# A fused routed-FFN, attention, routed-FFN block on one core: where the first gathers are issued, and in which pieces and order the attention's pipeline is filled

## The chip, the cores and the metric

The program runs on one core of a Trainium2 chip. The core has a matrix engine (TensorE, in the profile PE, its weight loads PEld), a vector engine (VectorE, DVE), an activation engine (ScalarE, ACT), GpSimd (POOL) and a queue engine (SyncE, SP). Each works through its own list of instructions in order and waits on semaphores. SP and ACT issue plain DMA transfers, POOL issues the indirect ones (gathers and scatters by row number). The metric is the device time of one execution in microseconds.

## The reference

The input x holds 32 sequences of 256 tokens of 128 numbers (8192 tokens). Three residual steps follow each other:

```python
x = x + 0.5 * ffn(layernorm(x), waff, W1, b1, W2, b2, threshold)
x = x + attn(layernorm(x), W_qkv, u_qkv, sigma_qkv, W_proj, u_proj, sigma_proj)
x = x + 0.5 * ffn(layernorm(x), waff, W1, b1, W2, b2, threshold)

# ffn: affinity of each token to 8 experts; one expert a token (argmax), kept where its
# rank within the sequence is below a capacity that comes from the mean affinity
dispatch = one_hot(argmax(aff)) * (ranks < cap)
for each expert: out += gelu((x * dispatch_e) @ W1_e + b1_e) @ W2_e + b2_e    # 128 -> 512 -> 128

# attn: 16 heads of 8, causal, softmax; weights scaled by spectral norms
qkv = sn_dense(x); att = softmax(mask(q k^T * 8**-0.5)); x = sn_dense(att v)
```

## The kernel before, in words

The program is a row of blocks: `token_stats` (layer norm statistics and affinities), `route("r1")` (which token goes to which slot), `experts("e1")`, `attention`, `experts("e2")`. At the end of a block every engine meets at a barrier (printed at the line of the block that comes next to it, here L496 for the end of `route`), then `Mem.clear` clears the semaphores and holds a second barrier (L66). No engine starts on the next block before both.

**The route and the first gathers.** VectorE makes in `gidx` the row numbers of 72 slot tiles (L798). POOL waits for it (`gidx_done`) and issues the gathers of the first two tiles (L577) within the `route` block. The rest of the tiles is gathered in `experts` (L867), in order on POOL. A tile is 128 rows of `rows`, two tiles are a pair and share one buffer `e_x`.

**The experts.** For pair i VectorE runs `keep(i)` (L1034, waits for both gathers of the pair), `norm` (L1045), and for each tile `fetch` (L1054), the copy of the tile's own expert's first weights into `e_w1own`. The list of VectorE holds `keep(5)` ahead of `fetch` for tile 6. TensorE transposes a pair (L972), expands each tile (L981), and contracts it (L992) some tiles later; ACT computes the gelu between (L936).

**The attention.** It is a pipeline over the 32 sequences in steps `turn(b)`, b from -4 to 35, each of twelve slots u = 0 to 11 on every engine. In turn b the work for several sequences is interleaved: sequence b+4 is gathered and normalised; sequence b+3 is projected to q and k (and v); the scores by query of sequence b+1 (its tiles 7 to 11, slots 0 to 4) and b+2 (its tiles 0 to 6, slots 5 to 11) are made for the row maxima only; for sequence b the scores by key are made, exponentiated (L1360), masked and multiplied by v. So the turns -4 to -1 fill the pipeline: turn -3 projects sequence 0, turn -2 projects sequence 1 and starts the maxima of sequence 0, turn -1 projects sequence 2, ends the maxima of sequence 0 and starts those of sequence 1, and turn 0 is the first with the scores by key.

The values q and k are carried as three bf16 parts. TensorE writes both to `mi[0]` (slot 2); ACT rounds them to the first part (L1371, `a_done`), VectorE takes the rest (L1697, `r_done`), ACT rounds it to the second part (L1380, `b_done`), and VectorE makes the third (L1711, `part_done`). SP then writes all of `part`, 192 KB in each of two transfers, to a buffer `qkd` in DRAM (L1226), and when they have landed reads it back in another layout: SP six transfers into `kb` (L1238), ACT six into `qs` (L1353). TensorE's first maxima tile of the sequence (L1430) waits for all twelve.

The row maxima of a sequence (VectorE's twelve reductions, L1678) are cut into three bf16 parts on POOL (L1328 to L1334), transposed on TensorE (L1552, slot 8, also in `mi[0]`), copied by ACT into `mt` (L1398) and written by SP into `qs` (L1231). The scores by key wait for that transfer (`m_in`).

In each turn SP holds, in this order: the transfers of `part` of sequence b+3, the maxima of sequence b+1, the reads into `kb`, and the rows of x.

## Time and profile before

| what | value |
|---|---|
| time, median of 3 runs | 1015.39 us (1014.93 to 1016.19) |
| profiled execution, its own time | 1012.83 us |
| its span | 1011.1 us |
| TensorE busy | 876.8 us, 87% of the span |
| VectorE busy | 748.7 us, 74% |
| GpSimd busy | 691.8 us, 68% |
| ScalarE busy | 599.8 us, 59% |

The busy time of an engine is the sum of its instructions without waits. The span is the part of the execution that the profiler records; the time of the execution includes what lies around it. In rows of the trace the first number is the start in microseconds from the span's start, the second the length; an `x6` behind a row says that six neighbours are merged, and square brackets give the idle time of the engine ahead of the row and what ended it.

### The profile page before, as it was taken

To read this page: it belongs to the slowest core of one execution; us is meant where nothing else is said; L and a number is where in the kernel's file an instruction comes from. 1 tells how busy PE (TensorE), PEld (TensorE's weight loads), DVE (VectorE), ACT (ScalarE), POOL (GpSimd) and SP (SyncE) were. 2 spreads that over 40 slices of the span, in tenths; PEclk is the share of its full clock that TensorE was granted. 3 is DMA by queue.
4 is the path that set the end of the run, shared out by engine and by line. 5 is a ranking of instruction groups with operands and counts; after the bars stand their busy time and mean duration, and the time that the engine had idled before them with its cause. 6 is when DMAs were issued, how large, how long until landed. Compare 5 with 4: busy or idle time off the path is not lost. (4 is left out here: it accounts for less than half of the span.)

```text
span 1011.1 us, 26251 instructions
## 1 busy us (share of the span) xinstructions
PE 876.8 (87%) x8024; PEld 664.9 (66%) x8057; DVE 748.7 (74%) x2500; ACT 599.8 (59%) x1575; POOL 691.8 (68%) x1245
## 2 busy tenths in 40 slices
PE   5936599999557999999999999999999974899995
PEld 5833499999524566565656566666666542899995
DVE  8879756555247789998998989898989854655552
ACT  2537466666314666666766666666666661666662
POOL 7709578753123678888888888888887774266664
PEclk9999889999858999999999999999999995899998
DMA  7450032222145553545464445455444301222220
GB/s 213 129 186 0 9 74 68 73 70 63 43 93 111 108 107 93 125 95 120 93 118 96 117 99 110 105 106 108 102 109 95 72 18 49 65 74 67 68 65 22
DMA packets 127017, 89.50 MB, mean 89 GB/s; under 512 B 14187, under 2 KB 117536, under 8 KB 126880
## 3 DMA queue, kind: packets, MB, share of 16 engines
q1 hardware_dynamic: 102752, 52.55, 22.9%
q10 hardware_dynamic: 15488, 17.74, 7.8%
q0 software_dynamic: 8640, 17.53, 6.7%
q8 instruction: 68, 1.11, 0.5%
q14 instruction: 69, 0.57, 0.2%
HBM read 52.09 MB, written 35.34 MB: 86 GB/s over the span
## 5 line engine op out<-in xcount | busy, mean ns | idle before, releaser
L1360 ACT ACTIVATE at_pt<-at_pm 128x512 f32<-128x512 f32 x384 | 228.0, 598 | 118.2 <-PE at_pm L1448 89.9
L1678 DVE TENSOR_REDUCE at_mx<-at_pp 128x2 f32<-128x512 f32 (+1 forms) x384 | 259.7, 679 | 43.0 <-PE at_pp L1437 35.7
L1276 POOL TENSOR_SCALAR_AFFINE_SELECT at_pt<-at_pt 128x256 f32<-128x256 f32 (+1 forms) x384 | 188.0, 493 | 57.1 <-ACT at_pt L1360 54.3
L936 ACT ACTIVATE e_ht<-e_ps_h,b1t 128x128 f32<-128x128 f32 x568 | 161.7, 370 | 84.2 <-PE e_ps_h L981 84.1
L981 PE MATMUL e_ps_h<-e_xnt,e_w1own 128*128 128x128 f32 x1136 | 153.3, 280 | 2.0 <-ACT e_xnt L930 1.3
L992 PE MATMUL e_ps_y<-w,e_ht 128*128 x1136 | 149.1, 275 | 0.0
L981 PEld LDWEIGHTS e_ps_h<-e_xnt,e_w1own 128*128 128x128 f32 x1136 | 141.0, 196 | 3.2 <-ACT e_xnt L930 2.0
L992 PEld LDWEIGHTS e_ps_y<-w,e_ht 128*128 128x128 f32 x1136 | 137.8, 192 | 0.0
L900 POOL DMA_INDIRECT out_dram<-e_y,e_x x71 | 82.3, 1159 | 68.1 <-DVE e_y L1062 51.9
L1062 DVE SCALAR_TENSOR_TENSOR e_y<-e_ps_y,e_x 128x256 f32<-128x256 f32 x72 | 30.3, 421 | 110.3 <-PE e_ps_y L992 110.3
L1469 PE MATMUL at_po<-at_pt,vp 128*32 128x256 f32 (+1 forms) x2048 | 109.8, 332 | 1.6 <-POOL at_pt L1276 1.6
L1435 PE MATMUL at_pp<-kb,qs 96*128 96x512 bf16 x256 | 100.1, 391 | 7.4 <-DVE at_mx L1678 6.2
L1448 PE MATMUL at_pm<-qs,kb 128*128 128x256 bf16 x512 | 97.7, 272 | 9.7 <-DMA qs<-at_mt 8.2
L867 POOL DMA_INDIRECT e_x<-rows,gidx x69 | 68.7, 995 | 38.8 <-DVE e_y L1062 21.3
L1469 PEld LDWEIGHTS at_po<-at_pt,vp 128*32 128x32 f32 x2048 | 53.4, 109 | 50.5 <-issue 21.0
L1448 PEld LDWEIGHTS at_pm<-qs,kb 128*128 128x128 bf16 x512 | 47.9, 97 | 48.1 <-DMA qs<-at_mt 15.5
L1322 POOL DMA_INDIRECT buckets<-at_x,at_to x64 | 65.4, 1022 | 20.0 <-issue 19.2
L1054 DVE COPY e_w1own<-w 128x512 f32 x142 | 64.7, 458 | 14.6 <-issue 9.3
L1283 POOL DMA_INDIRECT at_xa<-x,place x64 | 65.9, 1029 | 11.7 <-issue 11.3
L1437 PE MATMUL at_pp<-mask,identb 128*128 128x256 bf16 x256 | 70.9, 277 | 0.0
L1430 PE MATMUL at_pp<-kb,qs 96*128 96x256 bf16 x256 | 50.5, 279 | 7.6 <-DMA kb<-at_qkd 7.1
L1452 PE MATMUL at_pm<-qs,kb 128*128 128x128 bf16 x512 | 49.2, 218 | 2.8 <-ACT at_pt L1360 1.1
(324 smaller groups left out, 1744.5 us busy)
## 6 DMA issues: line engine op xcount, KB each, us to landing
at_qkd<-at_part SPq DMA_DIRECT2D x64, 192.0 KB, 3.0
kb<-at_qkd SPq DMA_DIRECT2D x64, 96.0 KB
qs<-at_qkd ACTq DMA_DIRECT2D x64, 96.0 KB
e_x<-buckets SPq DMA_DIRECT2D x71, 66.0 KB, 1.9
x<-e_y SPq DMA_DIRECT2D x35, 128.0 KB, 1.8
rows<-ts_x ACTq DMA_DIRECT2D x16, 264.0 KB, 3.0
ts_x<-in_x_dram SPq DMA_DIRECT2D x16, 256.0 KB, 3.3
x_by_token<-at_xa SPq DMA_DIRECT2D x32, 128.0 KB
```

The costliest lines, as they stand in the source:

```text
L867: pool.indirect_dma_start(x_row[s][:, j % 2, :], None, rows, bass.IndirectOffsetOnAxis(ap=c.gidx[:, j:j + 1], axis=0)).then_inc(x_in[s], 16)
L900: pool.indirect_dma_start(y_dram, bass.IndirectOffsetOnAxis(ap=to, axis=0), y_row[s][:, j % 2, :], None, bounds_check=T - 1, oob_is_err=Fa ...
L936: last = a.activation(hid_t[j % NB][:, f, :], ps_h[j % NB][:, f, :], ACT.Gelu, bias=c.b1t[:, ds(e, 1), f])
L981: last = te.matmul(ps_h[j % NB][:, f, :], w1_own[j % NB][:, f * P:(f + 1) * P], xn_t[(j // 2) % NX][:, j % 2, :], start=True, stop=True, s ...
L992: last = te.matmul(out, hid_t[j % NB][:, f, :], c.w2[:, ds(e, 1), f, :].rearrange("p a d -> p (a d)"), start=(f == 0), stop=(f == FC - 1))
L1276: g.affine_select(out=tile, in_=tile, compare_op=ALU.is_ge, fill=0.0, base=0, pattern=[[0, n], [1, P]], channel_multiplier=-1).then_inc(ma ...
L1360: a.activation(pt[u % RING][:, :], pm[u % 2], ACT.Exp, scale=SCALE).then_inc(exped, 1)
L1435: te.matmul(out, qs[s][0:ROWS, v - 4, P:S], kb[s][0:ROWS, v - 4, :, :].rearrange("p r q -> p (r q)"), start=True, stop=False, skip_group_c ...
L1437: te.matmul(out.rearrange("p (r q) -> p r q", r=2)[:, :, P:S], c.identb[:, :], c.mask[:, 0:2, :], start=False, stop=True, skip_group_check ...
L1448: last = te.matmul(out[:, i * S:(i + 1) * S], kb[s][:, g + 2 * w + i, r, 0:P], qs[s][:, g + 2 * w + i, :], start=True, stop=True)
L1469: last = te.matmul(out[32 * j:32 * j + 32, (half + 1) * S - cols:(half + 1) * S], values[:, w // 2, at:at + 32], src[:, i * cols:(i + 1) * ...
L1678: v.tensor_reduce(out, src, axis=AX.X, op=ALU.max).then_inc(maxed, 1)
```

## The change

Three things are changed, all of them at the start of a block.

First, the two gathers in `route` and their semaphore are gone, and `experts` issues all gathers.

Second, ACT makes one exponential of a single number at the very start of the attention's block. Nothing uses its value.

Third, the fill is ordered differently. For sequence 0 alone, `part` is written in pieces: the first parts when `a_done` is there, the second parts at `b_done`, the third parts at `part_done`, the last of these six transfers issued by ACT. Up to turn 0 VectorE makes the third parts ahead of the maxima tile in slot 5. In turn -1 the maxima of sequence 0 are transposed at the start of slot 5 instead of in slot 8, are copied by ACT in slot 5, and SP writes them ahead of the parts of sequence 2.

```diff
-            pool.wait_ge(gidx_done, 1)
-            for j in range(2 * HEAD_PAIRS):
-                pool.indirect_dma_start(c.x_row[j // 2][:, j % 2, :], None, io["rows"], ...)
...
-                for j in range(2 * HEAD_PAIRS, 2 * NR):
+                for j in range(2 * NR):
                     gather(j)
...
+            def maxima_in(b, k):
+                q = (k + 1) % NQ
+                wait(sp, mt_out, b + 2)
+                sp.dma_start(qs[q][ROWS:ROWS + 6, :, :], mt[q % 2][:, :].unsqueeze(1)).then_inc(m_in[q], 16)
...
+                    if n == 0:
+                        for done, s in ((a_done, slice(0, 6, 5)), (b_done, slice(1, 5, 3))):
+                            wait(sp, done, 1)
+                            for r in range(2):
+                                sp.dma_start(rows_out(h, r)[:, s, :], part[h][64 * r:64 * r + 64, s, :]).then_inc(piece_out, 16)
+                        wait(sp, part_done, 1)
+                        sp.dma_start(rows_out(h, 0)[:, 2:4, :], part[h][0:64, 2:4, :]).then_inc(part_out[h], 16)
+                    if b == -1:
+                        maxima_in(b, k)
+                    if n > 0:
+                        wait(sp, part_done, n + 1)
...
+            a.activation(cell[0:1, 7:8], c.part[0:1, 0:1], ACT.Exp, scale=-1.0).then_inc(early_exp, 1)
             act.wait_ge(zeroed, NZ)
...
+                    if u == 8 and b == -3:
+                        wait(act, part_done, 1)
+                        act.dma_start(rows_out(0, 1)[:, 2:4, :], part[0][64:P, 2:4, :]).then_inc(part_out[0], 16)
-                    if u == 8 and has(1):
+                    if u == (5 if b == -1 else 8) and has(1):
...
+                        if b == -1:
+                            wait(pe, mt_out, b + 2)
...
+                    if b == -1 and u == 5:
+                        wait(pe, r_done, b + 4)
+                        turn_maxima()
...
+                    if u == 5 and has(3) and b < 1:
+                        third_pieces(b, k)
                     for o, w in QUERY_TILES[u]:
```

On POOL, at the border of `route` and `experts`, the list before reads (L577 is in `route`, L496 and L65 are the border):

```order
L573 TENSOR_SCALAR qs<-r_iotab,r_colp 128x128 x48
L577 DMA e_x<-rows,gidx 128x132 x2
L496 UNCONDITIONAL_BRANCH
L65 ISA
L863 UNCONDITIONAL_BRANCH
L867 DMA e_x<-rows,gidx 128x132 x22
```

and now:

```order
L573 TENSOR_SCALAR qs<-r_iotab,r_colp 128x128 x48
L496 UNCONDITIONAL_BRANCH
L65 ISA
L859 UNCONDITIONAL_BRANCH
L863 DMA e_x<-rows,gidx 128x132 x24
```

The two gathers stand behind the border instead of ahead of it.

On TensorE, in turn -1 (kb0 and qs0 are sequence 0, kb1 and qs1 sequence 1, at_mp0 the cut maxima of sequence 0), before:

```order
L1435 MATMUL at_pp1<-kb0,qs0 128x512
L1437 MATMUL at_pp1<-mask,identb 128x2x128
L1430 MATMUL at_pp0<-kb1,qs1 128x256 x2
L1432 MATMUL at_pp0<-mask,identb 128x512
L1525 MATMUL at_mi0<-wv,at_xt0 128x128 x2
L1430 MATMUL at_pp1<-kb1,qs1 128x256 x2
L1432 MATMUL at_pp1<-mask,identb 128x512
L1430 MATMUL at_pp0<-kb1,qs1 128x256 x2
L1432 MATMUL at_pp0<-mask,identb 128x512
L1430 MATMUL at_pp1<-kb1,qs1 128x256 x2
L1432 MATMUL at_pp1<-mask,identb 128x512
L1552 MATMUL at_mi0<-identb,at_mp0 48x128 x2
```

and now:

```order
L1455 MATMUL at_pp1<-kb0,qs0 128x512
L1457 MATMUL at_pp1<-mask,identb 128x2x128
L1497 MATMUL at_mi0<-identb,at_mp0 48x128 x2
L1450 MATMUL at_pp0<-kb1,qs1 128x256 x2
L1452 MATMUL at_pp0<-mask,identb 128x512
L1554 MATMUL at_mi0<-wv,at_xt0 128x128 x2
```

The transposes of the maxima moved from behind four tiles of sequence 1 to ahead of the first.

On SP, in the attention's fill (kb0 to kb2 are the buffers of sequences 0 to 2, at_qkd0 and at_qkd1 the two DRAM buffers), before, without the reads of sequences 0 and 1 that stand between:

```order
L1226 DMA at_qkd0<-at_part0 64x6x256 x2
L1238 DMA kb0<-at_qkd0 24x8x256
...
L1226 DMA at_qkd1<-at_part1 64x6x256 x2
L1238 DMA kb1<-at_qkd1 24x8x256
...
L1241 DMA x1_by_token<-at_xa0 128x2x128
L1226 DMA at_qkd0<-at_part0 64x6x256 x2
L1231 DMA qs0<-at_mt0 6x8x256
L1238 DMA kb2<-at_qkd0 24x8x256
```

and now:

```order
L1231 DMA at_qkd0<-at_part0 64x2x256 x4
L1233 DMA at_qkd0<-at_part0 64x2x256
L1252 DMA kb0<-at_qkd0 24x8x256
...
L1241 DMA at_qkd1<-at_part1 64x6x256 x2
L1252 DMA kb1<-at_qkd1 24x8x256
...
L1255 DMA x1_by_token<-at_xa0 128x2x128
L1218 DMA qs0<-at_mt0 6x8x256
L1241 DMA at_qkd0<-at_part0 64x6x256 x2
L1252 DMA kb2<-at_qkd0 24x8x256
```

Sequence 0 goes out in five transfers from SP (the sixth is ACT's), and in turn -1 the maxima of sequence 0 and the parts of sequence 2 have changed places.

## Rows read from the trace of the kernel before

**Rows 1.** Stretches: start:end, length, busy time by engine (instructions), PEclk, DMA share, GB/s

```profile
310.00:316.50 6.50, 5.67 (x21) 1.84 (x20) 5.82 (x15) 0.45 (x2) 0.72 (x1) 0.50 0.45 110
333.50:337.00 3.50, 2.11 (x27) 1.42 (x20) 1.89 (x4) 2.10 (x5) 2.42 (x4) 1.00 0.44 97
440.00:800.00 360.00, 341.97 (x3502) 219.22 (x3524) 326.15 (x993) 240.10 (x520) 302.01 (x653) 1.00 0.49 105
```

**Rows 2.** Line L496, drains at the end of `route`: min/median/max ns, first and last start

```profile
L496 POOLq DRAIN  x1: 4502/4502/4502, 118.2 to 118.2; - x1
L496 DVEq DRAIN  x1: 10/10/10, 118.9 to 118.9; - x1
```

**Rows 3.** Timeline, start of the experts

```profile
124.12 0.95 POOL L867 DMA_INDIRECT e_x<-rows,gidx  x1 [3.14 <-POOLq L66]
125.23 0.14 DVE L1034 TENSOR_TENSOR e_x<-e_x,keep 128x2 f32<-128x2 f32 x1
128.72 3.78 PE L981 MATMUL e_ps_h<-e_xnt,e_w1own 128*128 128x128 f32 x16 [0.83 <-ACT e_xnt L930]
```

**Rows 4.** Timeline, the sixth pair in the experts

```profile
136.24 0.94 POOL L867 DMA_INDIRECT e_x<-rows,gidx  x1 [0.30 <-issue]
138.79 0.17 DVE L1034 TENSOR_TENSOR e_x<-e_x,keep 128x2 f32<-128x2 f32 x1 [1.35 <-DMA e_x<-rows,gidx]
138.90 0.43 DVE L1054 COPY e_w1own<-w 128x512 f32 x1
139.40 0.74 PEld L981 LDWEIGHTS e_ps_h<-e_xnt,e_w1own 128*128 128x128 f32 x6
```

**Rows 5.** Timeline, turns -3 and -2 of the attention

```profile
280.32 0.60 ACT L1371 ACTIVATE at_part<-at_mi 128x512 bf16<-128x512 f32 x1 [2.17 <-PE at_mi L1488]
282.33 0.69 DVE L1711 TENSOR_TENSOR at_part<-at_rest,at_part 128x512 bf16<-128x512 f32 x1 [0.69 <-ACT at_part L1380]
283.06 1.35 SPq L1226 DMA_DIRECT2D at_qkd<-at_part  x2
286.70 4.48 SPq L1238 DMA_DIRECT2D kb<-at_qkd  x6
293.33 0.63 ACT L1380 ACTIVATE at_part<-at_rest 128x512 bf16<-128x512 f32 x1 [0.76 <-DVE at_rest L1697]
294.31 0.61 PE L1430 MATMUL at_pp<-kb,qs 96*128 96x256 bf16 x2 [2.37 <-DMA kb<-at_qkd]
296.69 1.31 SPq L1226 DMA_DIRECT2D at_qkd<-at_part  x2
```

**Rows 6.** DMA issues of the page: KB each, median us from issue to landing

```profile
at_qkd<-at_part SPq DMA_DIRECT2D x64, 192.0 KB, 3.0
e_x<-buckets SPq DMA_DIRECT2D x71, 66.0 KB, 1.9
```

**Rows 7.** Timeline, turn -1 and the start of turn 0

```profile
306.24 0.68 DVE L1678 TENSOR_REDUCE at_mx<-at_pp 128x2 f32<-128x512 f32 x1
307.88 0.24 POOL L1334 TENSOR_TENSOR at_mp<-at_nr,at_mp 128x32 bf16<-128x32 f32 x1
310.29 1.31 SPq L1226 DMA_DIRECT2D at_qkd<-at_part  x2
313.89 4.32 SPq L1238 DMA_DIRECT2D kb<-at_qkd  x6
318.37 0.40 PE L1452 MATMUL at_pm<-qs,kb 128*128 128x128 bf16 x4 [0.92 <-ACT at_pt L1360]
321.28 0.11 PEld L1430 LDWEIGHTS at_pp<-kb,qs 96*128 96x128 bf16 x2 [0.69 <-DMA kb<-at_qkd]
```

**Rows 8.** Timeline, table load and SP in turn 0, a wait in turn 1

```profile
316.43 1.28 ACT L1360 ACT_TABLE_LOAD   x1 [3.71 <-issue]
326.40 0.81 SPq L1231 DMA_DIRECT2D qs<-at_mt  x1
335.82 0.11 PEld L1430 LDWEIGHTS at_pp<-kb,qs 96*128 96x128 bf16 x2 [1.61 <-DMA kb<-at_qkd]
```

More of the change, by code:

```diff
@@ L546, in route @@
         zeroed = sem("zeroed")
-        far_done, near_done, gidx_done = sem("far"), sem("near"), sem("gidx")
+        far_done, near_done = sem("far"), sem("near")
         NA = 2
@@ L1472, in times_v, with turn_maxima @@
                     last.then_inc(pv_done, 1)
+                def turn_maxima():
+                    wait(pe, mp_done, b + 2)
+                    for j in range(TPB):
+                        last = te.transpose(mi[0].bitcast(BF16)[0:3 * H, j * P:(j + 1) * P],
+                                            mp[(k + 1) % 2][:, j, :, :].rearrange("p t h -> p (t h)"), c.identb[:, :])
+                    last.then_inc(mt_tr, 1)
                 def small(u):
@@ L1659, in _, with third_pieces @@
             dve.wait_ge(made, NM)
+            def third_pieces(b, k):
+                q = (k + 1) % 2
+                wait(dve, b_done, b + 4)
+                v.tensor_tensor(part[q][:, 2:4, :], rest[q][:, :].rearrange("p (a n) -> p a n", a=2), part[q][:, 1:5:3, :],
+                                ALU.subtract).then_inc(part_done, 1)
             def turn(b, k, has):
@@ L1707, in turn @@
                                         ALU.mult).then_inc(on_done, 1)
-                    if u == 5 and has(3):
-                        q = (k + 1) % 2
-                        wait(dve, b_done, b + 4)
-                        v.tensor_tensor(part[q][:, 2:4, :], rest[q][:, :].rearrange("p (a n) -> p a n", a=2), part[q][:, 1:5:3, :],
-                                        ALU.subtract).then_inc(part_done, 1)
+                    if u == 5 and has(3) and b >= 1:
+                        third_pieces(b, k)
                     if u == 6 and has(4):
```

36 lines of the change are left out of this document (16 added, 20 removed).

## The prediction

> **What bounds the kernel now.** I read the stretches first, then the chain of waits, then the timeline at the borders of the blocks. In the steady part of the attention TensorE is busy 341.97 of 360 us at its full clock, and VectorE 326.15 [rows 1]. In the experts TensorE's instructions stand back to back. So whatever starts the experts or the attention earlier shifts all that follows by as much, as long as TensorE is not starved a moment later; and an instruction that is removed in the steady part is not what this change is about. The change works on two borders: the end of the route, and the attention's fill (turns -4 to 0), where TensorE waits for transfers several times.
>
> At the end of the route VectorE is the last to compute; its drain stands at 118.9. POOL's drain starts at 118.2 and lasts 4.50 us, to 122.7: it holds the barrier until the gathers that POOL has issued are through [rows 2]. In the fill the chain runs from the parts of a sequence (SP's write) through DRAM to the reads into `kb`, to TensorE's first maxima tile. TensorE is found waiting for `kb` at 294.31, 321.28 and 335.82 [rows 5, 7, 8].
>
> **Part one, the gathers.** Removed from the route: two gathers on POOL, and with them the long drain. The barrier is then VectorE's: 118.9 in place of 122.7, so all engines enter the experts 3.8 us earlier. Added in the experts: the same two gathers, ahead of the fourteen others that are issued without a wait. One gather follows another after 0.94 + 0.30 = 1.25 us [rows 4]. POOL's first one moves from 124.12 [rows 3] to 120.3; the third, which was the first there, comes 2 x 1.25 later, at 122.8. So each later gather is 3.8 - 2.5 = 1.3 us earlier.
>
> Who waits for them? The first pair: its second gather ends at 120.3 + 1.25 + 0.94 = 122.5, and a gather's data is there 1.6 us after that (136.24 + 0.94 to 138.79 [rows 4]), so at 124.1. Before, `keep` for the first pair ran at 125.23, held by VectorE's own start and not by data [rows 3]. Thus TensorE's first expansion, at 128.72 before, could start up to 2.3 us earlier. But not all of it lasts. At 138.79 `keep(5)` waited 1.35 us for its gathers, the copy of tile 6's weights stands behind it on VectorE and ends at 139.33, and TensorE takes that tile at 139.40 [rows 4]: a margin of under 0.1 us. This wait now comes 1.3 us earlier, not 2.3, and TensorE waits for the difference. After this pair POOL gains on TensorE (2.5 us a pair against four tile steps of 0.9, some 3.8), so nothing further is lost. Part one: **-1.3 us**. The ends of its range: -0.9 if the two gathers, which come first in a block, take 0.2 us more each (my allowance), and -2.3 if the wait at `keep(5)` gives way.
>
> **Part two, the fill.** I take the times in the frame of before, with the attention's start fixed.
>
> *Pieces of sequence 0.* Before, both transfers wait for the third part: issued from 283.06 on over 1.35 us, landed at 286.70 when the reads begin [rows 5], 2.9 us after the second's start. Now the first parts are ready at 280.92 and the second at about 282.3 (where the third begins) [rows 5]. The trace shows no transfer of this shape. Its issue on SP is bounded by 0.81 us for the 24 KB of maxima [rows 8] and 0.68 for 192 KB (half of 1.35), 0.75 for a read (a sixth of 4.48) [rows 5]; below I allow 0.4, since a third of the runs of data is left. At 0.65 SP issues from 280.96 to 282.25, from 282.35 to 283.65, and the last at 283.65; ACT's comes beside it. That is hardly earlier than the second transfer before (283.73); the rest must come from size. A 66 KB read lands in 1.9 us, a write of 192 KB in 3.0 [rows 6]. With 2.15 us for a write of 64 KB, nearer to the row of its size, the reads start at 285.8: **-0.9 us**, between -0.2 (it lands no faster for being small) and -1.2 (issues at 0.4 us).
>
> A rule speaks against this. The Trainium skill, "DMA: Bandwidth & Descriptors", section "Rules for kernel authors", says that many small transfers should be joined, since under 64 KB one pays mostly overhead; its section on the anatomy of one DMA puts the fixed part at about 2.0 us plus bytes over 436 GB/s. By that estimate a piece of 64 KB lands in 2.15 us and one of 192 KB in 2.45, a gain of only 0.3; the rows have 1.1 us between the two sizes, and the sum goes by the rows.
>
> *Third parts first.* In turn -2 the second part of sequence 1 is ready at 293.96, but its write starts at 296.69 [rows 5], because VectorE first had the maxima tile that waits for `kb`. Now the write starts at 293.96 - 0.9 + 0.75 = 293.85, which is 2.8 us earlier. The tile behind it on VectorE arrives on TensorE only at 294.31 - 0.9, so the 0.68 us of the third part cost nothing. The reads for sequence 1 land 2.8 us earlier too, and ACT, which issues six of them, is free sooner for the copy of sequence 2.
>
> *Maxima in turn -1.* They end at 306.92 before, the cutting on POOL at 308.12 [rows 7]. What leads to them starts with TensorE's first tile of sequence 0 (-0.9) and runs through ACT, now unblocked: -1.1, so the cut maxima are there at 307.0. TensorE now waits for them ahead of the first tile of sequence 1, whose reads, issued from 297.45 on and as long on the way as those of sequence 0 (7.6 us), have landed at about 305.1. So what the reads gain is not all used: queued behind the transposes are the seven tiles of sequence 1, and they start at 307.45. ACT copies at 307.5, SP writes at 307.95 for 0.8 us, and only then, at 308.75, the parts of sequence 2, in place of 310.29 [rows 7]: **-1.5 us**, although they were ready at 306.6. The reads of sequence 2 start at 312.35 (before 313.89).
>
> *Turn 0.* The first scores by key come 1.8 us earlier. The table load of 1.28 us ahead of the first exponential [rows 8] now lies at the attention's start, where ACT does nothing until the first copy of sequence 0; together with ACT's earlier reads TensorE's step at 318.37, which waited for ACT, comes 2.8 us earlier. But the next tile that needs new data, at 321.28, already waited 0.69 us for `kb` [rows 7]; its data is 1.5 us earlier and no more. TensorE waits there 1.7 us instead, and of the 2.8 us 1.5 are left. So the early table costs nothing and by itself yields nothing: the wait for the reads of sequence 2 takes its place. In turn 0 SP reads sequence 3 only after the write of sequence 1's maxima, which ended at 327.21 [rows 8] and follows TensorE, also -1.5; the wait of 1.61 us at 335.82 stays as it is. Part two: **-1.5 us**, from -0.8 (pieces at -0.2) to -2.8 (the read of sequence 2 is not what binds).
>
> **Sum.** -1.3 - 1.5 = -2.8 us: the profiled execution goes from 1012.83 to 1010.0. The median of the runs is 2.56 us above that execution, so 1015.39 becomes **1012.6**.
>
> **Rivals.**
>
> *A, the gains are real but half as large* (chance 0.2). The two gathers cost 1.45 us each and the pieces land no faster than the whole: -0.9 - 0.8 = -1.7, giving 1013.7. For it: the pieces' last issue is at the time of the old one. Against it: the 1.1 us between the sizes.
>
> *B, TensorE isn't held by the next wait* (0.15). `keep(5)` slips by less, and the reads land earlier because the DMA engines are less crowded: -2.3 - 2.8 = -5.1, giving 1010.3. Against it is the margin of 0.1 us at 139.40; for it, that the six reads of sequence 0 needed 7.6 us from issue to the first tile and those of sequence 2 7.4, under a load that may change.
>
> *C, the clock falls in turn 0 and the kernel is slower* (0.1). From 310 to 316.5 TensorE was granted 0.50, that is 1.2 GHz of 2.4, after TensorE had sat idle for the reads of sequence 1 [rows 1]. The new wait of 1.7 us at 319 follows soon on the slow stretch. If the clock stays low there, every slow microsecond costs half: 6.5 us cost 3.3, and the result is 1015.39 - 2.8 + 3.3 = 1015.9. It decides against the change from 5.6 us of slow clock on, and needs 9.7 for a loss that counts. Against it: a wait of 1.61 us at 335.82 left the clock at 1.00 [rows 1, 8].
>
> *D, the whole fill is hidden* (0.05): TensorE is short of work in turns 1 and 2 anyway and gives all of part two back; 1014.1.
>
> **The numbers.** My own case has 0.5, with a range of 1011.8 to 1013.6. All cases but the far ends of B and C lie between 1010.5 and 1014.9, the edge on the slow side reaching past A and D. A measurement of this kernel tells about 0.2% (2.0 us) from no change. My case gives faster in nine of ten, B always, A and D scarcely, C never, which with D's and A's remainder gives 0.65 faster, 0.28 the same, 0.07 slower, the last from C and from what I have not seen.
>
> **What would show it.** POOL's drain at the route's end under 1 us and the first gather near 120.3; the first expansion near 126.4, then a wait of about 1 us of TensorE ahead of tile 6, held by the sixth pair's gathers. In the attention, counted from its start: reads of sequence 0 0.9 us earlier, the write of sequence 1 2.8, of sequence 2 1.5; no table load in turn 0; a longer wait for `kb` in turn 0. I would be wrong if the barrier does not follow VectorE, if the pieces land together as late as before, if TensorE's clock in turn 0 is below 1, or if the distance from turn 0 to the attention's end grows.

## The result, and the profile after

The changed kernel takes 1012.05 us, the median of 13 runs (1008.74 to 1014.03), and the kernel before 1015.39 (13 runs, 1013.31 to 1017.54). The ratio of the two is 0.9970, with a 95% interval of 0.9961 to 0.9980. On another chip the same pair gave 1012.73 and 1015.54, ratio 0.9971, interval 0.9961 to 0.9982 (e12 below). So the change makes the kernel 2.8 to 3.3 us faster; 2.8 had been forecast. The profiled execution of the changed kernel took 1011.68 us with a span of 1009.9.

Positions are compared below as distances from an event that both kernels have: in the experts from the end of the last instruction that VectorE computes in the route (the cast into `eid`: 118.64 before, 119.33 after), in the attention from POOL's first gather into `at_xa` (270.73 before, 270.04 after). Such a distance is written with a plus sign, +14.96. Line numbers differ between the kernels.

**The border of the route.** The drains of L496 in the changed kernel, which answer to [rows 2] (count, min/median/max ns, first and last start):

```profile
L496 POOLq DRAIN  x1: 9174/9174/9174, 102.5 to 102.5; - x1
L496 DVEq DRAIN  x1: 10/10/10, 119.6 to 119.6; - x1
```

POOL's drain is not shorter, it is longer: 9.17 us. But it begins at 102.5, while POOL's last work of the route (L573) is still running, and ends at 111.7, as that work does, well ahead of VectorE. What counts is when a drain ends, not how long it is. The barrier is now VectorE's.

The start of the experts and the sixth pair in the changed kernel, which answer to [rows 3] and [rows 4]:

```profile
120.32 1.28 ACT L936 ACT_TABLE_LOAD   x1 [7.04 <-PEq L66]
121.11 1.24 POOL L863 DMA_INDIRECT e_x<-rows,gidx  x1 [9.47 <-POOLq L66]
123.92 0.94 POOL L863 DMA_INDIRECT e_x<-rows,gidx  x1 [0.30 <-issue]
125.30 0.16 DVE L1030 TENSOR_TENSOR e_x<-e_x,keep 128x2 f32<-128x2 f32 x1 [3.17 <-DMA e_x<-rows,gidx]
127.16 1.22 PE L977 MATMUL e_ps_h<-e_xnt,e_w1own 128*128 128x128 f32 x4 [0.47 <-ACT e_xnt L926]
...
135.46 0.95 POOL L863 DMA_INDIRECT e_x<-rows,gidx  x1 [0.31 <-issue]
138.14 0.16 DVE L1030 TENSOR_TENSOR e_x<-e_x,keep 128x2 f32<-128x2 f32 x1 [1.51 <-DMA e_x<-rows,gidx]
138.26 0.43 DVE L1050 COPY e_w1own<-w 128x512 f32 x1
138.79 0.91 PE L977 MATMUL e_ps_h<-e_xnt,e_w1own 128*128 128x128 f32 x6 [0.72 <-ACT e_xnt L926]
```

Read the releasers. `keep` for the first pair is now held by its gathers for 3.17 us, where before VectorE's own start held it. TensorE's first expansion stands at +7.83 in place of +10.08, 2.25 us earlier. At tile 6 TensorE sits idle for 0.72 us, and there was no such gap before. The row names ACT's copy of `e_xnt` as the releaser, but the copy of tile 6's weights ends at 138.69, only 0.1 us ahead of TensorE, and it stands behind `keep(5)`, which waited 1.51 us for gathers. From here on to the attention everything is 1.3 to 1.4 us earlier: the attention starts at +150.71, before at +152.09.

Look at POOL as well. The third gather starts at +4.59 (123.92), before at +5.48 (124.12): 0.89 us earlier. The twelfth, the last that `keep(5)` needs, starts at +16.13 (135.46), before at +17.60 (136.24): 1.47 us earlier. The difference of 0.58 us is not made by the change: the nine gathers between, the same in both kernels, took that much less in this profile.

**The fill of the attention.** Timeline of the changed kernel, which answers to [rows 5], [rows 7] and [rows 8]:

```profile
269.27 1.28 ACT L1358 ACT_TABLE_LOAD   x1 [5.67 <-PEq L66]
280.25 2.63 SPq L1231 DMA_DIRECT2D at_qkd<-at_part  x4
282.36 0.68 ACTq L1413 DMA_DIRECT2D at_qkd<-at_part  x1
282.92 0.61 SPq L1233 DMA_DIRECT2D at_qkd<-at_part  x1
285.00 4.56 SPq L1252 DMA_DIRECT2D kb<-at_qkd  x6
292.65 0.69 DVE L1692 TENSOR_TENSOR at_part<-at_rest,at_part 128x512 bf16<-128x512 f32 x1 [0.69 <-ACT at_part L1397]
293.37 1.30 SPq L1241 DMA_DIRECT2D at_qkd<-at_part  x2
...
304.95 0.73 DVE L1692 TENSOR_TENSOR at_part<-at_rest,at_part 128x512 bf16<-128x512 f32 x1
306.53 0.27 PE L1497 MATMUL at_mi<-identb,at_mp 128*48 128x128 bf16 x2 [3.27 <-POOL at_mp L1348]
306.73 0.39 PE L1450 MATMUL at_pp<-kb,qs 96*128 96x256 bf16 x2
307.24 0.78 SPq L1218 DMA_DIRECT2D qs<-at_mt  x1
308.12 1.32 SPq L1241 DMA_DIRECT2D at_qkd<-at_part  x2
311.74 4.34 SPq L1252 DMA_DIRECT2D kb<-at_qkd  x6
313.48 0.63 PE L1468 MATMUL at_pm<-qs,kb 128*128 128x256 bf16 x2
...
319.41 0.39 PE L1450 MATMUL at_pp<-kb,qs 96*128 96x256 bf16 x2 [1.41 <-DMA kb<-at_qkd]
333.28 0.11 PEld L1450 LDWEIGHTS at_pp<-kb,qs 96*128 96x128 bf16 x2 [0.28 <-DMA kb<-at_qkd]
```

The last piece of sequence 0 is issued at 282.92 and the reads begin at 285.00: 2.1 us, where the whole half took 2.9. The third part of sequence 1 is ready ahead of the maxima tile, and its write follows at once. In turn -1 a new gap appears, the one that matters most below: TensorE waits 3.27 us for the cut maxima at 306.53, and SP holds back the parts of sequence 2, ready at 305.68, until 308.12. The first tile of sequence 1 stands at 306.73 (+36.69, before +37.60), the first scores by key at 313.48 (+43.44, before +44.52). The same stretches as in [rows 1], the first two moved to the same distance from the attention's start:

```profile
309.31:315.81 6.50, 6.22 (x25) 2.62 (x26) 5.52 (x14) 1.21 (x3) 1.14 (x2) 0.55 0.65 145
332.81:336.31 3.50, 3.44 (x39) 2.47 (x38) 2.65 (x6) 2.59 (x6) 2.72 (x6) 1.00 0.16 41
440.00:800.00 360.00, 340.98 (x3504) 220.03 (x3526) 325.89 (x996) 241.16 (x522) 302.30 (x652) 1.00 0.48 105
```

The steady part is as before. The half clock in the first stretch is still there in this profile (0.55, before 0.50), and the clock does not fall in turn 0.

A caution on the end. The table load of the last experts stands 588.44 us behind the attention's start, before 588.74: of a fill that is 1.5 us shorter this pair of profiles shows 0.3 at the end. The steady turns differ by more than that from one execution to the next. The reads of the last sequence stand at +515.98, +519.08 and +517.44 in the three profiles with the old fill (before, e1, e3; mean 517.5), and at +515.06, +516.61, +516.06, +516.70 and +516.54 in five with the new one (after, e2, e4, e9, e12; mean 516.2). The means differ by 1.3 us, but the three old ones alone spread over 3.1, so the profiles point to a gain that is carried to the end and do not show it by themselves. The times do: the fill alone has a ratio below 1 over its whole interval (e2), if only just. For single steps I rely on positions in the fill, and on times only where an interval speaks. The positions spread too: the reads of sequence 2 stand at +43.16, +43.70 and +44.84 in the three profiles with the old fill, and at +41.70 to +42.04 in the five with the new one. Against the profile of before the gain there is 1.46 us, between the means 2.0.

### The profile page after: what moved, and what is told of

It reads as the page before. It is cut to its first block and busy times, and to the rows that moved or that the text cites. A ratio compares the mean times of both kernels' runs of the same rounds, so it can differ in the third digit from the quotient of the medians.

```text
span 1009.9 us, 26259 instructions
## 1 busy us (share of the span) xinstructions
PE 876.5 (87%) x8024; PEld 665.2 (66%) x8057; DVE 748.7 (74%) x2500; ACT 600.8 (59%) x1576; POOL 691.7 (68%) x1245
```

## The experiments

All times are device microseconds. The ratio is to the kernel before on the same chip, with its 95% interval. Three chips were used: e1 to e4 ran on one (before: 1016.29), e5 to e8 on a second (1027.81), e9 to e12 on a third (1015.54). On the second the profiles show TensorE, ACT and VectorE standing still for some 12 us in all in the first experts, much of it released by nothing that the profile shows, and the kernel before took 12 us longer there too; positions counted from the attention's start don't contain it.

### e1: the gathers alone

The kernel before with part one only (no gathers in `route`, all 24 in `experts`).

> The kernel before with only the gathers moved into the experts. Theory (the barrier follows VectorE, then the sixth pair's gathers hold TensorE): POOL's drain at the route's end under 0.1 us, all engines in the experts 3.7 us earlier, the first expansion 2.1 us earlier counted from the end of the route's last VectorE instruction, tile 6 only 1.3 us earlier, and the attention's start 1.3 us earlier; time -1.3 us (ratio 0.9987). Rival B (TensorE is not held at tile 6): the attention's start 2.1 to 2.3 us earlier. Rival that the barrier's gain is void: no shift. The attention's fill has the positions of before, counted from its start.

Measured: 1015.79 us, ratio 0.9993 (0.9982 to 1.0004). ACT's first instruction of the experts stands at +1.00, the first expansion at +7.82, the gap at tile 6 is 0.65 us, and the attention starts at +150.87 in place of +152.09: 1.22 us earlier. Up to the attention's start the positions agree with the theory, but the third gather is 0.90 us earlier and not 1.3 (+4.58); the twelfth, at +16.43, is 1.17 earlier. The fill does not have the positions of before, as was expected: it is unchanged, and yet its write of sequence 1 comes 0.81 us later than in the profile of before, its reads of sequence 2 1.68 later, and those of sequence 6 3.0. That is the spread spoken of above. The time can't tell 1.2 us from nothing.

### e2: the fill alone

The kernel before with the parts two and three of the change.

> The changed kernel with the two gathers back in the route: only the fill's edits are left. Theory: the experts as before (tile 6 without a wait), the attention's positions those of the changed kernel: the first read of sequence 0 1.0 us earlier counted from the attention's start, of sequence 2 1.4, the wait for kb in turn 0 about 1.4 us. If the fill lasts, time -1.5 us (0.9985); if the later turns take back what they took in the profile of the changed kernel, -0.9 us.

Measured: 1015.08 us, ratio 0.9987 (0.9975 to 0.9999). The experts are as before (first expansion +10.07, attention +152.10). Reads of sequence 0 at +15.03, write of sequence 1 at +23.30, reads of sequence 2 at +41.98, of sequence 3 at +55.88. The fill of the changed kernel is reproduced without the experts' part. By the positions the two parts are independent; the two ratios multiply to 0.9980, against 0.9970 measured for both, each uncertain by 0.0010 to 0.0012, so the times allow it and no more.

### e3: one gather left in the route

```diff
-            for j in range(2 * HEAD_PAIRS):
+            for j in range(1):
...
-                for j in range(2 * HEAD_PAIRS, 2 * NR):
+                for j in range(1, 2 * NR):
```

> The kernel before with one gather in the route and the other in the experts. It parts the two things that come with the first edit: the earlier start of the block, and the place of the gathers in POOL's list. POOL's drain should end 1.25 us earlier, and so should the experts' start; but POOL then has one more gather there, so that all gathers from the third on stand where they stood. Theory (the gathers set TensorE's time at tile 6): tile 6 and the attention's start are unmoved within 0.2 us, time 0. Rival (the block's start sets it): 1.25 us earlier, ratio 0.9988.

Measured: 1017.39 us, ratio 1.0000 (0.9988 to 1.0011). L496 in this kernel:

```profile
L496 POOLq DRAIN  x1: 3179/3179/3179, 118.3 to 118.3; - x1
```

With one gather in flight the drain is 3.18 us, with two 4.50 [rows 2]: each gather adds about one gather's issue, and in both the drain ends 1.7 us after the record of the last gather. The engines enter 1.3 us earlier than before, the first expansion is 1.3 earlier (+8.76), but POOL still has to issue the gather that it gave up, so that the third gather is where it was (+5.42, before +5.48). The attention starts at +151.71, 0.38 us earlier, where 0.2 at most was expected by the theory and 1.25 by the rival. That is far nearer to the theory, and the rest has a likely source: the twelfth gather came 0.57 us earlier (+17.03), because the gathers ahead of it were shorter. So what counts in the end is the time of the sixth pair's gathers, not the time at which the engines enter.

### e4: the weights of tile 6 ahead of keep(5)

The changed kernel, with `fetch(6)` taken out of its place behind `keep(5)` and put ahead of it:

```diff
+                if by_slot and i == 1:
+                    fetch(6, e[6])
                 if i + NORM < NU:
                     keep(i + NORM)
```

> The changed kernel with the copy of tile 6's weights ahead of the wait for the sixth pair's gathers on VectorE, in the first experts only. Theory: TensorE's wait of 0.72 us at tile 6 is due to that order alone; it goes, TensorE's later tiles and the attention's start come 0.7 us earlier, time -0.7 us against the changed kernel. Rival: the sixth pair's rows themselves are needed as soon (the transposes of the pair wait): the wait moves to the next transposes and nothing is gained.

Measured: 1014.24 us, ratio 0.9979 (0.9966 to 0.9992). The gap at tile 6 is gone, and the transposes of the sixth pair come at +22.57 in place of +23.10. But the attention starts at +151.27, not earlier than +150.71. The loss is at the tenth pair. Timeline of e4, POOL, VectorE and TensorE, and then the same place in the changed kernel:

```profile
152.50 2.14 DVE L1050 COPY e_w1own<-w 128x512 f32 x1
152.53 1.83 POOL L873 MEMSET kb<- 96x2048 f32 x1
154.75 1.13 PE L977 MATMUL e_ps_h<-e_xnt,e_w1own 128*128 128x128 f32 x8 [0.68 <-issue]
```

```profile
151.70 1.83 POOL L873 MEMSET kb<- 96x2048 f32 x1
152.63 1.19 DVE L1050 COPY e_w1own<-w 128x512 f32 x1
...
155.99 1.82 POOL L873 MEMSET kb<- 96x2048 f32 x1
156.78 1.31 DVE L1050 COPY e_w1own<-w 128x512 f32 x1 [0.27 <-issue]
```

A copy of this shape takes 0.42 us. These take 2.14, 1.19 and 1.31, and each ends 0.28 to 0.29 us after the memset that POOL is running. VectorE's copy and POOL's memset don't overlap: the copy is held until the memset is through. In e4 the copy is wanted 0.03 us ahead of the memset by the records, and loses all of it. (The Trainium skill, "SBUF — State Buffer", section "Who interferes with whom", states such a lock between VectorE's instructions in a two-port mode and GpSimd, held for a whole instruction by whoever issues first. The rows agree on the lock; on the order they show a copy with the earlier start waiting. Whether this copy runs in such a mode, no trace here says.) So a wait was removed and given back 16 us later, by a collision that the new time brought about.

### e5: sequence 0 written whole

The changed kernel, with the write of sequence 0 as before (two transfers of 192 KB at `part_done`).

> The changed kernel, but sequence 0 is written as before, in two transfers of 192 KB when the third parts are there. Counted from the attention's first gather, the changed kernel's pieces are written from 10.21 to 12.88 and its reads begin at 14.96, those of before at 15.97. Theory of the prediction (a small write lands sooner): reads of sequence 0 at 15.9 to 16.0, first maxima tile about 1.0 later, and so the write of the maxima and of sequence 2's parts about 1.0 later (39.1); the attention ends 1 us later. Rival (the pieces buy nothing downstream, because the cut maxima come from ACT and VectorE, which have slack): reads later by 1.0, but sequence 2's parts within 0.3 of 38.08.

Measured: 1026.81 us, ratio 0.9992 (0.9979 to 1.0005). Timeline of e5 (its attention starts at 282.53):

```profile
298.58 4.48 SPq L1243 DMA_DIRECT2D kb<-at_qkd  x6
306.57 0.61 PE L1436 MATMUL at_pp<-kb,qs 96*128 96x256 bf16 x2 [2.77 <-DMA kb<-at_qkd]
```

Reads at +16.05 in place of +14.96, the first maxima tile at +24.04 in place of +22.72, the maxima of sequence 0 at +38.91 in place of +37.20, the reads of sequence 2 at +43.43 in place of +41.70. Within the fill the theory holds, and the rival (slack downstream) does not: the loss of 1.1 us at the reads is still there in turn -1. That it grows to 1.7 is not the edit's doing alone. In e7 and e8, whose fill is that of the changed kernel up to there, the last maxima tile of sequence 0 also comes 1.0 us later on this chip (+33.7 in place of +32.73). Beside e6, the profile of this chip nearest to the changed kernel, the loss is 0.97 at the reads of sequence 0, 1.31 at the maxima and 1.32 at the reads of sequence 2. That the attention ends 1 us later is not seen: at the reads of sequence 4 the loss against e6 is 0.1 (e6 has a stop of its own ahead of them), and the last sequence, at +515.78, stands where it does in the changed kernel. The chip has no run of the changed kernel beside it, so only the positions speak here.

### e6: without the early exponential

> The changed kernel without the early exponential: the table is loaded ahead of the first exponential again (1.28 us). Theory of the prediction: the first exponential comes 1.3 later than 44.25, the wait of TensorE for kb at 49.4 shrinks from 1.7 to about 0.4 or less, and what follows that tile stands where it was: 0 us. Rival (the table load is on the path): the tile itself slips by 1.28 and with it all that follows: +1.3 us.

The one line with `early_exp` is left out. Measured: 1026.31 us, ratio 0.9987 (0.9975 to 0.9999). Timeline of e6 (its attention starts at 282.97):

```profile
328.08 1.28 ACT L1376 ACT_TABLE_LOAD   x1 [5.70 <-issue]
332.92 0.11 PEld L1449 LDWEIGHTS at_pp<-kb,qs 96*128 96x128 bf16 x2 [0.68 <-DMA kb<-at_qkd]
```

The first exponential comes at +46.40 in place of +44.25 to +44.61, the wait of TensorE for `kb` shrinks to 0.68 us from 1.69 to 2.09, and the tile that ends it stands at +49.95; in the profiles of after, e2, e9 and e12 it stands at +49.36, +49.90, +49.90 and +49.76. What the table load costs, the wait for the reads gives back, all but a few tenths: the early table yields next to nothing, as predicted. (Turn 1 of this profile is then 1.0 to 1.6 us later, behind one stop of TensorE of 1.51 us at +65 that the profile puts down to nothing, as those in the experts on this chip.)

### e7: the maxima of turn -1 late again

The changed kernel, with the transposes of the maxima in turn -1 in slot 8 and SP's write of them behind the parts of sequence 2, as before the change. Pieces, early third parts and early table stay.

```diff
-                    if b == -1:
-                        maxima_in(b, k)
...
-                    if b == -1 and u == 5:
-                        wait(pe, r_done, b + 4)
-                        turn_maxima()
```

> The changed kernel, but in turn -1 the maxima of sequence 0 are transposed in slot 8 and written behind the parts of sequence 2, as before. Theory (the reads of sequence 2 bind turn 0, and SP writes the maxima ahead of them in either order): parts of sequence 2 written at about 35.7 in place of 38.08, maxima only at 39.5 to 41, so the reads of sequence 2 at 40.5 to 41.8 (changed kernel 41.70), the first scores by key 1.5 to 2.5 later than 43.44; TensorE waits less for kb, and the tile of sequence 2 comes within 0.5 of the changed kernel's 51.05: 0 us, so that the third part ahead of the tile alone brings what the write order seems to bring. Rival (early maxima are what shortens the fill): everything from turn 0 on 1.3 us or more later.

Measured: 1024.72 us, ratio 0.9978 (0.9965 to 0.9990), the lowest on its chip. Timeline of e7 (its attention starts at 281.83):

```profile
316.81 0.39 PE L1448 MATMUL at_pp<-kb,qs 96*128 96x256 bf16 x2 [0.76 <-DMA kb<-at_qkd]
318.49 1.30 SPq L1239 DMA_DIRECT2D at_qkd<-at_part  x2
320.99 0.81 SPq L1218 DMA_DIRECT2D qs<-at_mt  x1
322.10 4.31 SPq L1250 DMA_DIRECT2D kb<-at_qkd  x6
323.49 0.39 PE L1466 MATMUL at_pm<-qs,kb 128*128 128x256 bf16 x2
329.75 0.39 PE L1448 MATMUL at_pp<-kb,qs 96*128 96x256 bf16 x2 [1.95 <-DMA kb<-at_qkd]
```

The maxima are written 2.0 us later (+39.16), a little ahead of what was expected. But the first scores by key come at +41.66, which is 1.8 us **earlier** than in the changed kernel (+43.44), and the reads of sequences 2, 3 and 4 at +40.27, +53.89 and +68.97 in place of +41.70, +55.34 and +70.47. Neither the theory (no change) nor the rival (later) had this. The reads of sequence 2 come earlier because SP no longer waits for the maxima ahead of the parts: these are written at +36.66 in place of +38.08. The scores come earlier because TensorE starts the seven tiles of sequence 1 at +34.98 in place of +36.69, 1.71 us earlier: nothing in its queue waits for the maxima any more. It also runs them at the full clock. The stretch of 6.5 us from +39.27 in e7 (the granted clock is the third number from the right):

```profile
321.10:327.60 6.50, 5.57 (x33) 2.81 (x32) 5.32 (x10) 2.71 (x6) 2.38 (x5) 1.00 0.69 139
```

A pair of matmuls takes 0.39 us here, and 0.61 to 0.64 from the third tile on in the changed kernel, where this stretch was granted 0.55. But the clock explains next to nothing here. From the first tile of sequence 1 to the first scores it takes 6.68 us in e7 at the full clock, 6.75 in the changed kernel, 6.69 in e8 at 0.50, and 6.89 in e12 at 0.86. The tiles wait for VectorE's reductions of 0.68 us each, and VectorE is busy for 5.32 to 6.21 of the 6.50 us. It is not always so cheap: in e1 and e3 (old order) the half clock was there from the first tile on, whose two matmuls took 0.61 us, and the same way took 7.9 us, against 6.92 in the kernel before. So by the positions the change's early maxima cost 1.4 us of the fill; what they are meant to shorten they make longer. The time does not show it by itself: no run of the changed kernel stands on this chip, the nearest, e6, has a median 1.6 us higher, and the two intervals overlap.

### e8: ACT writes the maxima of turn -1

The changed kernel, with the maxima transposed early as there, but written by ACT right behind its copy, so that SP is free for the parts of sequence 2.

> The changed kernel, but in turn -1 ACT writes the maxima of sequence 0 itself, right behind its copy, so that SP need not wait for them and writes the parts of sequence 2 when they are ready (305.68 in the trace of the changed kernel, where they were written at 308.12). Theory (the reads of sequence 2 are what TensorE waits for in turn 0): parts written at about 35.7 in place of 38.08, reads at 39.3 in place of 41.70, no wait for kb of 1.4 to 1.7 us at 49.4; the attention from there on 1.4 us earlier. Rival one (another wait takes its place in turn 0 or 1, by ACT or the maxima): the wait goes but the tiles that follow stand within 0.3 of where they were. Rival two (ACT's DMA of 0.8 us sits ahead of its copies and costs as much): first scores by key 0.8 later, total unchanged or later.

Measured: 1025.61 us, ratio 0.9981 (0.9970 to 0.9993). The stretch from +39.27; then the first tile of sequence 1, the first scores by key and the wait in turn 1:

```profile
320.56:327.06 6.50, 5.88 (x20) 2.19 (x20) 5.66 (x14) 1.09 (x3) 0.76 (x2) 0.50 0.69 137
```

```profile
319.00 0.39 PE L1451 MATMUL at_pp<-kb,qs 96*128 96x256 bf16 x2
325.69 0.63 PE L1469 MATMUL at_pm<-qs,kb 128*128 128x256 bf16 x2
345.01 0.39 PE L1451 MATMUL at_pp<-kb,qs 96*128 96x256 bf16 x2 [1.00 <-DMA kb<-at_qkd]
```

Parts of sequence 2 written at +36.68, reads at +40.29, no wait for `kb` in turn 0: SP's part of the theory is right. But TensorE still waits 3.27 us for the maxima, its first tile of sequence 1 stands at +37.71, the first scores come at +44.40, and the reads of sequence 3 at +55.04, 1.15 later than in e7 with the same start of the reads of sequence 2. A wait of 1.0 to 1.3 us comes up in turn 1. This is rival one. Rival two had the first scores later too, and they are, by 0.96 us against the changed kernel; but TensorE is 1.0 us late already at the last tile of sequence 0 (+33.74 in place of +32.73), which this edit does not touch. Its matmuls there took 0.61 us each for 4 us longer than in the changed kernel. e7 stands at the same place (+33.72), so e7 and e8 can be compared, and together they say that of SP's gain in sequence 2 most is lost again by sequence 3 when TensorE's queue waits for the maxima.

### e9: the clears of kb in halves

e4 had shown the collision. Each of the four buffers `kb` is cleared by POOL within the experts, behind a pair of gathers, in 1.83 us. Here each clear is cut in two, behind two different pairs:

```diff
-                if what == 0:
-                    g.memset(c.kb[k][0:ROWS, :, :, :].bitcast(F32), 0.0)
+                if what <= 0:
+                    m = n % 2
+                    k = n // 2
+                    g.memset(c.kb[k][0:ROWS, 4 * m:4 * m + 4, :, :].bitcast(F32), 0.0)
```

> The changed kernel, but POOL clears each kb buffer in the experts in two halves, behind two different pairs, in place of one memset of 1.83 us behind one pair. In every trace so far VectorE's copy of 0.42 us that comes up during such a memset ends 0.28 us after it (copies of 1.19 to 1.35 us, 2.14 us once), and the three pairs behind the first memset are 4.2 to 4.3 us apart on TensorE in place of 3.79: 1.4 us. Theory (the memset holds VectorE's copy up, and a half of 0.92 us ends before the copy is wanted): copies below 0.7 us, pairs 8 to 13 all 3.8 apart, the distance from pair 8 to pair 13 19.0 in place of 20.4, and 1.4 us less in all. Rival (POOL is what is short: two gathers and a memset are 4.3 us a pair, and splitting it only spreads the loss): the distance from pair 8 to pair 18 stays at 39.3.

Measured: 1010.77 us, ratio 0.9957 (0.9942 to 0.9972); the changed kernel on the same chip 1012.73, ratio 0.9971. Timeline of e9:

```profile
158.66 0.97 POOL L875 MEMSET kb<- 96x1024 f32 x1
159.86 0.42 DVE L1052 COPY e_w1own<-w 128x512 f32 x1
```

The half ends before the copy is wanted. From the transposes of pair 8 to those of pair 13 it is 18.96 us (32.86 to 51.82) in place of 20.36 (32.69 to 53.05): 1.40 us, as expected; the attention starts at +149.50, 1.2 us earlier than in e12. The rival (POOL is short of time) is out: the pairs behind are 3.79 apart as well. The kernel before has the same loss, so this is not part of the change, but a gain of its own.

### e10: three edits together

The changed kernel with the edits of e4, e7 and e9.

> The changed kernel with three edits: fetch of tile 6 ahead of keep(5) (as in e4), the clears in halves (as in e9), and the maxima of turn -1 in slot 8 again, behind the parts of sequence 2 (as in e7). Theory: the edits add up. The sixth pair's wait is gone (0.4 to 0.7), 1.4 from the clears, reads of sequence 2 at 40.3 and of sequence 3 at 53.9 in place of 41.7 and 55.3 counted from the attention's start (1.4): 3.2 to 3.5 us less than the changed kernel on the same chip, ratio to before near 0.994. Rival (the fetch in its new place meets a clear as in e4, or the earlier experts bring POOL's gathers back as the limit): 2.5 us or less.

Measured: 1009.72 us, ratio 0.9949 (0.9936 to 0.9963), 3.0 us below the changed kernel on the same chip and 5.8 below the kernel before. The attention starts at +148.91, 1.8 us earlier than in e12, and its reads of sequences 2 and 3 stand at +39.75 and +52.11, 2.2 and 3.6 us earlier. Timeline of turn -1 and the start of turn 0, and the whole stretch of the clock:

```profile
304.23 0.39 PE L1453 MATMUL at_pp<-kb,qs 96*128 96x256 bf16 x2 [2.36 <-DMA kb<-at_qkd]
315.01 0.39 PE L1453 MATMUL at_pp<-kb,qs 96*128 96x256 bf16 x2 [0.44 <-DMA kb<-at_qkd]
```

```profile
307.00:316.00 9.00, 7.00 (x46) 4.07 (x47) 7.70 (x17) 4.69 (x10) 3.94 (x7) 1.00 0.57 143
```

Again no half clock, this time behind 2.36 us of idle time, and the wait for `kb` in turn 0 is down to 0.44 us. The edits add up to the size forecast, a little below its range by the medians (3.0 for 3.2 to 3.5). Against e9, which differs by the edits of e4 and e7, it is 1.05 us, where 1.8 to 2.1 had been expected; with six runs each that is neither shown nor ruled out. One copy still meets a clear as in e4 (1.28 us, at 152.80). The profiled execution, 1007.48 us, was the fastest of six, and I don't read its steady turns as a further gain.

### e11: the third parts late again

The changed kernel with the third parts behind the maxima tile of slot 5 in every turn.

> The changed kernel, but the third parts are made behind the maxima tile of slot 5 in every turn, as before. Theory of the prediction for the write of sequence 1 (2.8 us earlier, of which 0.9 from sequence 0 and the rest from this order): write of sequence 1 at 25.0 to 25.2 in place of 23.33, its reads at 28.7. TensorE's first tile of sequence 1 then waits for them again in turn -1, and the parts of sequence 2 come 0 to 0.5 later than 38.08. Rival (the third parts decide more than the write they belong to): parts of sequence 2 and all that follows 1 us or more later.

Measured: 1014.76 us, ratio 0.9993 (0.9981 to 1.0004), 2.0 us above the changed kernel on the same chip. Timeline of e11 (its attention starts at 269.54):

```profile
293.96 0.68 DVE L1692 TENSOR_TENSOR at_part<-at_rest,at_part 128x512 bf16<-128x512 f32 x1
294.67 1.31 SPq L1241 DMA_DIRECT2D at_qkd<-at_part  x2
```

The write of sequence 1 goes back to +25.13, 1.7 us later, as expected. The parts of sequence 2 come 0.83 later than in e12 (+39.17), between theory and rival, and of this 0.44 is left at the reads of sequence 3 and 0.25 at those of sequence 7. That fits a loss of a few tenths, but the medians say 2.0. In the profile the rest appears in one turn far behind the fill (sequence 29 at +485.70, in e12 +483.68). I can't say why; whether a later third part makes such turns more frequent stays open.

### e12: the changed kernel once more

> The changed kernel once more, on the chip of the three others, to compare them with it directly and to see how far two profiled executions of one kernel agree. Expected: the positions of the fill within 0.3 us of the first profile up to the reads of sequence 2 (14.96, 26.94, 41.70), the ratio to before within 0.1% of 0.997.

Measured: 1012.73 us, ratio 0.9971 (0.9961 to 0.9982). Reads of sequences 0, 1 and 2 at +15.04, +26.99 and +41.95 (first profile +14.96, +26.94, +41.70), the attention at +150.69 (+150.71). Up to here two profiles of one kernel agree within 0.25 us; at the last sequence they are 1.5 us apart.

## Why the prediction was right, and where it was not

**The barrier.** Right: the engines enter the experts 3.85 us earlier (ACT at +0.99 in place of +4.84), 3.8 was predicted. The measure that I named for it was wrong: the drain is 9.17 us long, not under 1, and simply ends early.

**The gathers.** Right in the mechanism, and the size has luck in it. The first expansion came 2.25 us earlier (predicted 2.3), and the wait ahead of tile 6 took back 0.9 to 1.0 of it (predicted 1.0). The term of -1.3 measured -1.38, and -1.22 in e1. e3 and e4 show the mechanism from both sides. But the working had each later gather 1.3 us earlier, and the third is 0.9 earlier in every profile with all gathers in the experts (+4.58 or +4.59, before +5.48). POOL starts 3.7 us earlier and not 3.8, and the two gathers take 2.8 us and not 2.5, as the first is 1.24 long and not 0.94. That is the near end of the range that was given. The rest came from the nine gathers up to the twelfth: beyond the usual 0.94 us each they took 0.91 us in all in the profile of before, 0.61 in e2, 0.40 in e3, and 0.32 to 0.64 in the others. With those of before, the term would have been about -0.8 (an estimate: 1.38 less 0.57). Whether they are shorter by chance stays open.

**Pieces of sequence 0.** Right: -0.9 was predicted at the reads, -1.0 measured. The small last write lands 2.1 us after its issue (I had taken 2.15), and e5, where the last write is issued only 0.2 us later and lands 1.1 later, shows that the gain comes from how this write is cut and not from the time of its issue. Size alone does not set such times: the page of before has `x<-e_y`, 128 KB, at 1.8 us. The sum of the Trainium skill that I weighed against this ("DMA: Bandwidth & Descriptors", section "Anatomy of one DMA — SWDGE (gpsimd) path") would have given 0.3 us; the page states it for transfers that GpSimd issues, and these are SP's and ACT's, so it is no test of it. The runs decide for the rows.

**Third parts first.** Right: the write of sequence 1 is 2.63 us earlier (2.8 predicted), and e11 gives 1.7 of it to this order.

**Maxima in turn -1.** The sum was right and the step was not. I predicted the parts of sequence 2 1.5 us earlier, and they are 1.48 earlier; but I gave the 1.5 as what the move of the maxima yields. e7 shows that with the maxima left in their old place the reads of sequence 2 come a further 1.4 us earlier. The third part made ahead of the tile and the pieces bring all of the gain, and the move takes back half. The working even held the clue, "although they were ready at 306.6". What failed is the comparison: I compared with the kernel before, in which the parts were late anyway, and not with the same change without this one edit. I also missed what a waiting instruction at the head of TensorE's queue costs: the seven tiles behind it started 1.7 us later than they could (+36.69, in e7 +34.98).

**Turn 0.** The wait for `kb` of 1.7 us was predicted and measures 1.69 (weights) or 1.41 (matmul). The first scores by key came 1.1 us earlier and not 1.8: the tile from which they follow, the first of sequence 1, is only 0.9 earlier, as the prediction itself had it (307.45 for 308.33), and the seven tiles take 6.75 us where they took 6.92. TensorE's step at 318.37 came 2.1 us earlier and not 2.8. That the early table yields next to nothing is confirmed by e6.

**Turn 1.** Wrong in a detail: the wait of 1.61 us at 335.82 [rows 8] was to stay and is 0.28 us, because the reads of sequence 3 took 7.9 us and not 8.6. In turn 2 the same reads took 8.9 us where they had taken 8.1, and the tile that waits for them is 1.0 us earlier (+79.35 for +80.35), so about a third of the 1.5 is gone there; in e2, e4, e9 and e12 it is 0.6 to 1.2 earlier. One of the prediction's signs of being wrong did show in this pair of profiles: from the first scores by key to the attention's end it is 545.0 us, before 544.2. The spread above is larger than that.

**The rivals.** A (half the gain) is out by the positions, and the interval of the ratio (-2.0 to -4.0 us) leaves its -1.7 out. B (TensorE not held) is out: both waits that I named came. C (the clock falls in turn 0) did not happen: from +46 to +62 TensorE was granted 1.00 in the changed kernel, e2, e4, e9 and e12. Its price, half of every slow microsecond, depends on the place. In turn -1 of the changed kernel the tiles kept VectorE's pace at half clock and lost less than 0.1 us against e7; in e1 and e3 it cost about 1 us. D (all hidden) is hard to tell from a gain by the profiles; the interval of e2 (-0.1 to -2.5 us) leaves zero out, narrowly.

## What to carry to other kernels

Gathers that are issued just ahead of a barrier held this barrier until they were through. Issue such work just behind it, and then look for the next consumer that was on time by a tenth of a microsecond, because that one sets what is left of the gain. When a forecast comes out right, check its terms at the places that it names: here the third gather missed its place by 0.4 us, and other gathers made up for it. When a change has several edits in one chain, price each against the others in place, not against the kernel before: here one edit took back half of what its neighbours brought and the sum still looked as forecast. An instruction that waits at the head of an in-order queue costs the ready work behind it. And a slow clock costs little where another engine sets the pace: look first at what the tiles wait for.

## What the runs showed of the hardware

- POOL's drain at the end of `route` lasts until the gathers are through: 4.50 us with two just issued, 3.18 with one, each ending 1.7 us after the last gather's record, and off the path with none.
- The first gather behind the barrier took 1.24 us in the changed kernel where most take 0.94.
- VectorE's copy of 128x512 f32 (0.42 us) that comes up while POOL clears memory ends 0.28 us after the memset, whatever is left of it: 1.19, 1.31, 1.70 and 2.14 us. In the first experts this cost 1.4 us in the kernel before and in the changed one; with the memsets cut in halves of 0.97 us it was gone in e9.
- The write of `part` to DRAM let its waiter go after 2.1 us with 64 KB, after 2.9 to 3.0 with 192 KB.
- TensorE's granted clock in the 6.5 us from +39.27 was 0.54 to 0.96 in the profiles whose order of work there is that of the changed kernel (0.55, 0.96 in e2, 0.83 in e4, 0.54 in e5, 0.76 in e6, 0.54 in e9, 0.85 in e11, 0.86 in e12), 0.50 in e8, and 1.00 in e7 and e10. So two executions of one program need not get the same clock there. TensorE had been idle for 3.3 us ahead of turn -1's work in the changed kernel, e8 and e12, for 0.76 in e7 and for 2.36 in e10; whether that sets the clock is not shown.
- The time from the first tile of sequence 1 to the first scores by key did not follow this clock: 6.75 us at 0.55, 6.69 at 0.50 (e8), 6.89 at 0.86 (e12), 6.68 at 1.00 (e7). With the half clock from the first tile on, in e1 and e3, it was 7.9.
